# A Mamba, FFN, attention and MoE kernel: the first expert block's gate and up products beside the last chunk of the scan

## Chip, cores and metric

The kernel runs on one core of a Trainium2 chip. The metric is the device time of one execution in microseconds. Before the change: median 803.87 us of three runs (802.72 to 805.54). The engines are TensorE (PE in the profile), VectorE (DVE), ScalarE (ACT), GpSimd (POOL) and SyncE (SP, which here issues all DMAs).

## What is computed

Four layers, each as x = x + layernorm(layer(layernorm(x))), on x of 2 x 512 x 512 (b = batch). Only the first two are near the change:

```python
# layer 1: selective scan, 1024 channels of 16 states
state = state * exp(dt_t[..., None] * A) + (dt_t * u_t)[..., None] * B_t[:, None, :]
y = einsum('bdn,bn->bd', state, C_t)
out = ((y + x * D) * silu(gate)) @ W_out.T
# layer 2: FFN, 512 -> 1376 -> 512, 4 bit weights with scales s and zero points z (groups of 128)
w = q * s - (z + 1) * s          # for Wg, Wu and Wd
inter = silu(x2 @ Wg) * (x2 @ Wu)
out = (inter @ Wd).astype(float16)
```

Layer 3 is an attention over the 16 head dimensions of a token, layer 4 a MoE block whose experts are one shared weight, so that it comes down to products with folded weights.

## The kernel before

**The scan.** 1024 channels times two batches are 16 chunks of 128 channels (cc = 0 to 15, b = cc // 8). A chunk is 8 pairs (i = 0 to 127 in all, q = i % 8), and a pair is a 128 x 1024 tile of decays and states. Per pair ScalarE makes the decay by exp into PSUM (L1889), GpSimd the product dbu = rep_du * bc (L2397, up to three pairs ahead: it waits for the scan of pair i before the product of i + 3), VectorE the recurrence (`tensor_tensor_scan`, L1228), then VectorE (L1239) or, for two or three pairs of a chunk, GpSimd (L2406) the product with C, and TensorE sums two pairs at a time into the bank of y (L979). Once a chunk, one pair into the next chunk, VectorE multiplies y into the gate (`take_y`, L1255), for which TensorE then starts the next y with the product of u and D (L968).

**Other work in the scan** is put by hand. The table SIDE (L80) gives for chunk and pair of pairs what TensorE does ahead of its sums there; ScalarE and VectorE do their part of it a few pairs later (`pair_of(item) + n`). In chunks 13 and 14 stand the four transposes of the FFN's normalised input of batch 0 (`tr`, with `high_turned` on ScalarE and `low_turned` at L1318 on VectorE), in chunks 14 and 15 the partial output products of the scan layer (`part`, `take_partial`). In the last chunk `out_ahead` (L838) adds the second to last term of three output tiles, and `out_last` (L844) the last one behind the last `take_y`. All these products use a ring of three PSUM banks in the order of `pe_order` (L132).

**The FFN.** 1376 is padded to 11 blocks of 128 (IC). Weights are kept as two float16 halves, high and low, and a product is three matmuls (high x high, low x high, high x low, L721), 12 matmuls for a gate or up product of a block. Making a block's weights takes a chain: DMA of packed words, zero points and scales to one of four slots (`stage`, L627), `unpack` on VectorE (L1271), `whole` on ScalarE (cast to float16, L2163), then for blocks 0 and 1 `less_zero` (L1285) and products with scales split in two (`gate_up_halves`, `down_halves`, L1290 to L1296), and for the others `scaled` (L1278, L1280), `high_weights` on ScalarE (L2169) and `low_weights` on VectorE (L1300, L1305). In the pass of batch 0, TensorE does per block i gate and up, then the down product of block i - 1 (`down`, L992), which waits for `it_lo` (`ffn_low`, L1459). VectorE's order is written out: `unpack(0)`, `unpack(1)` and the last `take_y` close the scan (L1437), then L1560 to L1572, then the loop at L1573. `ffn_silu` (L2190), `ffn_times` (L1449) and `ffn_high` (L2197) stand between up product and `it_lo`. The next pass, of batch 1, uses the finished weights.

SyncE's queue has stage(0) in chunk 11, stage(1) behind the stores of wr, stage(2) behind the last `take_y`, stage(3) behind `out_last`, the others behind the low weights of the slot's user. Then come the loads for attention, bqraw among them (L674), and for the MoE block.

SBUF is laid out by hand in kilobytes (`at`, L209).

## Time and profile before

| | |
|---|---|
| median of three runs | 803.87 us |
| the profiled execution | 808.16 us, its span 806.3 us |
| mean granted TensorE clock | 0.907 of 2.4 GHz |
| busy: TensorE, VectorE, ScalarE, GpSimd | 689.0, 685.0, 469.9, 481.4 us |
| scan (VectorE's first to last) | 57.1 to 480.7 us |
| first gate product of the FFN | 489.7 us |
| last down product of its first pass | up to 579.1 us |

All times in the rows below are microseconds from the start of the span of this one execution, unless marked ns. A row of the timeline is: start, duration, engine, line of the kernel, operation, output and inputs by the program's names, shapes, count, and in brackets the idle time before it and what ended it. The granted clock is given as a share of 2.4 GHz; 0.50 is 1.2 GHz.

### The profile page before, as it was taken

The numbers are of one execution on the slowest core, as the hardware profiler recorded it, in microseconds if no ns is written. First come the engines' busy times: TensorE is split into PE (matmuls) and PEld (weight loads), VectorE is DVE, ScalarE is ACT, GpSimd is POOL, SyncE is SP. The second block draws the span as 40 slices with busy tenths as digits, with TensorE's granted clock in tenths as the row PEclk, the third lists the DMA queues.
The fourth block names the chain that finished last, engine by engine and source line by source line (L and its number), as shares of the span: only waits on it lengthen the run. The fifth ranks groups of instructions, "written<-read, shape, count | busy, mean of one in ns | idle before, by whom it ended". The sixth has DMA issues, their size and how long they took to land. (4 is left out here: it accounts for less than half of the span.)

```text
span 806.3 us, 8451 instructions
## 1 busy us (share of the span) xinstructions
PE 689.0 (85%) x2794; PEld 326.7 (41%) x2794; DVE 685.0 (85%) x697; ACT 469.9 (58%) x805; POOL 481.4 (60%) x252
## 2 busy tenths in 40 slices
PE   7979889987787799456646889999999999999995
PEld 7623333322122233111111224444444556887885
DVE  6879999999999989999999998999275575585778
ACT  5478768885656765867664546767235346323333
POOL 2429999999999999999999970220002014341130
PEclk9989979999788899856865988999999999999998
DMA  7533232335503705730334409973040030000011
GB/s 234 121 106 136 82 118 76 118 130 168 197 4 117 246 29 170 228 131 26 105 130 150 131 1 249 259 199 93 1 157 1 1 105 0 1 1 1 0 53 52
DMA packets 42358, 83.19 MB, mean 103 GB/s; under 512 B 6825, under 2 KB 10340, under 8 KB 42060
## 3 DMA queue, kind: packets, MB, share of 16 engines
q1 hardware_dynamic: 42316, 82.67, 32.4%
q8 instruction: 22, 0.36, 0.2%
q14 instruction: 20, 0.16, 0.1%
HBM read 71.44 MB, written 11.21 MB: 103 GB/s over the span
## 5 line engine op out<-in xcount | busy, mean ns | idle before, releaser
L2397 POOL TENSOR_TENSOR dbu<-rep_du,bc 128x1024 f32<-128x1024 f32 x127 | 296.5, 2361 | 2.5 <-DMA bc<-bc_scratch 1.2
L1889 ACT ACTIVATE psum<-rep_dt,aneg 128x512 f32<-128x512 f32 x256 | 166.3, 682 | 117.8 <-DVE hc L1239 96.3
L1228 DVE TENSOR_TENSOR_SCAN psum<-psum,dbu 128x1024 f32<-128x1024 f32 x89 | 203.3, 2285 | 3.0 <-ACT psum L1889 1.6
L979 PE MATMUL psum<-hc,stk 128*32 128x512 f32 x512 | 84.6, 743 | 54.5 <-POOL hc L2406 39.7
L1239 DVE TENSOR_TENSOR hc<-psum,bc 128x1024 f32<-128x1024 f32 x89 | 108.9, 1224 | 3.1
L2406 POOL TENSOR_TENSOR hc<-hc,bc 128x1024 f32<-128x1024 f32 x39 | 91.9, 2356 | 9.9 <-DVE hc L1228 9.9
L1228 DVE TENSOR_TENSOR_SCAN hc<-psum,dbu 128x1024 f32<-128x1024 f32 x39 | 88.9, 2280 | 5.5 <-PE psum L979 4.3
L718 PE MATMUL psum<-xf_hi,gu_hi 128*128 128x512 f16 x176 | 66.7, 379 | 0.1
L718 PE MATMUL psum<-xf_hi,gu_lo 128*128 128x512 f16 x176 | 66.7, 379 | 0.0
L718 PE MATMUL psum<-xf_lo,gu_hi 128*128 128x512 f16 x176 | 66.7, 379 | 0.0
L718 PE MATMUL psum<-xT,w_g 128*128 128x512 f32 x120 | 59.1, 641 | 2.6 <-ACT rep_du L2034 2.6
L2474 POOL TENSOR_TENSOR h<-h 128x512 f32<-128x512 f32 x16 | 19.4, 1213 | 68.0 <-ACT h L2305 68.0
L979 PEld LDWEIGHTS psum<-hc,stk 128*32 128x32 f32 x512 | 13.3, 120 | 109.8 <-issue 65.2
L968 PE MATMUL psum<-u,diag 128*32 128x512 f32 x128 | 23.5, 816 | 32.3 <-DVE u L1255 22.4
L2197 ACT CAST it_hi<-it 128x512 f16<-128x512 f32 x22 | 13.6, 618 | 48.1 <-DVE it L1449 48.0
L1449 DVE TENSOR_TENSOR it<-sg,psum 128x512 f32<-128x512 f32 x22 | 15.0, 684 | 29.2 <-PE psum L718 14.4
L718 PEld LDWEIGHTS psum<-xT,w_g 128*128 128x128 f32 x120 | 23.3, 204 | 40.0 <-issue 35.9
L2458 POOL TENSOR_TENSOR w_up_lo<-w_up,w_up_hi 128x1024 fp32r<-128x1024 f32 x4 | 9.4, 2388 | 46.2 <-ACT w_up_hi L2182 46.2
L718 PE MATMUL psum<-xT,w_x 128*128 128x512 f32 x64 | 32.6, 657 | 2.5 <-ACT xT L1773 2.0
L2445 POOL TENSOR_TENSOR x<-x,obuf 128x512 f32<-128x512 f32 x4 | 9.3, 2348 | 41.4 <-ACT obuf L1956 41.4
L1006 PE MATMUL psum<-d_hi,it_hi 128*128 128x512 f16 x88 | 33.3, 379 | 0.6 <-DVE it_lo L1459 0.6
L2452 POOL TENSOR_TENSOR w_gate_lo<-w_gate,w_gate_hi 128x32 fp32r<-128x32 f32 x1 | 0.7, 693 | 55.4 <-ACT w_gate_hi L2271 55.4
(301 smaller groups left out, 1455.2 us busy)
## 6 DMA issues: line engine op xcount, KB each, us to landing
rep_dt<-rep_scratch SPq DMA_DIRECT2D x60, 256.0 KB, 3.5
rep_du<-rep_scratch SPq DMA_DIRECT2D x60, 256.0 KB, 4.4
cw<-c_scratch SPq DMA_DIRECT2D x11, 768.0 KB, 8.1
qw<-qgu_in SPq DMA_DIRECT2D x11, 512.0 KB, 6.2
bc<-bc_scratch SPq DMA_DIRECT2D x16, 256.0 KB, 4.8
rep_scratch<-du_t SPq DMA_DIRECT2D x14, 256.0 KB, 2.0
rep_scratch<-dt_t SPq DMA_DIRECT2D x14, 256.0 KB, 2.3
qw<-qd_in SPq DMA_DIRECT2D x11, 256.0 KB, 7.1
```

Of the source, the lines that this page charges most:

```text
L718: last = pe.matmul(bank(item)[0:rows, cols], lhsT, rhs, start=(n == 0), stop=(n == len(parts) - 1))
L968: last = pe.matmul(y_rows(k), diag[:, k * P // KH:(k + 1) * P // KH], u[b][:, c, :], start=True, stop=False)
L979: last = pe.matmul(y_rows(k), stk[:], hc[:, (i + k // 2) % HCS, k % 2, :], start=False, stop=(s == GN - 1))
L1006: last = pe.matmul(psum[:, t, :], v, w, start=(i == 0 and n == 0), stop=(i == IC - 1 and n == 2))
L1228: dve.tensor_tensor_scan(h, a, dbu[:, i % DBS].rearrange("p e t -> p (e t)"), 0.0, ALU.mult, ALU.add)\
L1239: dve.tensor_tensor(hc[:, i % HCS], psum[:, two, :], bc[:, GN + n, :].unsqueeze(1).broadcast_to([P, 2, L]), ALU.mult)\
L1449: dve.tensor_tensor(it[:, k % 2, :], sg[:, k % 2, :], bank(("u", b, i)), ALU.mult)\
L1889: last = act.activation(psum[:, 2 * (i % 2) + e, :], rep_dt[:, cc % 2, k, :], ACT.Exp, scale=aneg[:, k, c, n:n + 1])
L2197: act.copy(it_hi[:, k % 2, :], it[:, k % 2, :]).then_inc(ithi_done, 1)
L2397: pool.tensor_tensor(dbu[:, i % DBS], rep_du[:, cc % 2, k:k + 2, :], bc[:, n, :].unsqueeze(1).broadcast_to([P, 2, L]), ALU.mult).then_inc( ...
L2406: pool.tensor_tensor(hc[:, i % HCS], hc[:, i % HCS], bc[:, GN + n, :].unsqueeze(1).broadcast_to([P, 2, L]), ALU.mult)\
L2474: pool.tensor_tensor(h2[:, k % 2, :], h1[:, k % 2, :], h1[:, k % 2, :], ALU.mult)\
```

## The change

The gate and up product of block 0, batch 0, move from the FFN's loop to chunk 15 of the scan. For that:

- VectorE does unpack(0) after pair 107 (13 * 8 + 3), less_zero(0) after 113, the two high halves of the gate and up weights after 115 and the low ones after 117. ScalarE casts the block's words after the decay of pair 110. The weights go to buffers of their own (hi_early, lo_early), since gu_hi and gu_lo of the block overlap buffers that the scan uses; so does the cast (q16_early).
- TensorE does the gate product ahead of the sums of pairs 120 and 121 and the up product ahead of those of 124 and 125. ScalarE copies the results to SBUF (sg_early, it_early) after pairs 124 and 127.
- After the scan: VectorE no longer unpacks block 0 there, and makes that block's down halves ahead of the last take_y. The order of the partial sums and weights of block 1 is another; the product of gate and up (times_early) comes between them. ScalarE's silu of block 0 runs from SBUF right after its table load.
- bqraw moves to another place in SBUF, and its load behind the wait for 10 releases of q16.

```diff
+UNPACK_AT = 13 * QP + 3
+WHOLE_AT = 13 * QP + 6
+HALVES_AT = 14 * QP + 1
@@ SIDE
-        (14, 1): [("part", 0)], (14, 2): [("part", 1)], (14, 3): [("part", 2)], (15, 1): [("part", 3)]}
+        (14, 1): [("part", 0)], (14, 2): [("part", 1)], (14, 3): [("part", 2)], (15, 0): [("g", 0, 0)],
+        (15, 1): [("part", 3)], (15, 2): [("u", 0, 0)]}
@@ buffers
+        q16_early = at("q16_early", 199, [SZ], F16)
+        hi_early = [at(f"hi_early{h}", k, [KH * P], F16) for h, k in enumerate([58, 170])]
+        lo_early = at("lo_early", 139, [2 * KH * P], F16)
+        sg_early = at("sg_early", 195, [L])
+        it_early = at("it_early", 197, [L])
-        bqraw = at("bqraw", 139, [DH, NH])
+        bqraw = at("bqraw", 203, [DH, NH])
@@ SyncE, behind the other loads for attention
+            sp_.wait_ge(q16_used, IC - 1)
+            load(bqraw[:].rearrange("p b c -> p (b c)"), bq_in.broadcast_to([P, DH * NH]), ld_att)
@@ TensorE, in the scan's loop
+                        if item[0] == "g":
+                            for t in range(NT):
+                                wait_taken(pe, ("tr", "ffn", 0, t))
+                            pe.wait_ge(whi_first, 1)
+                            pe.wait_ge(wlo_gu, 1)
+                        if item[0] in ("g", "u"):
+                            gate_or_up(*item)
@@ VectorE
+            def early_high():
+                for h in range(2):
+                    n = slice(h * KH * P, (h + 1) * KH * P)
+                    last = dve.tensor_tensor(hi_early[h][:], cw[0][:, 0, n], cw[0][:, 1, n], ALU.mult)
+                last.then_inc(whi_first, 1)
+
+            def early_low():
+                n = slice(0, 2 * KH * P)
+                dve.tensor_tensor(lo_early[:], cw[0][:, 0, n], cs[0][:, n], ALU.mult).then_inc(wlo_gu, 1)
+
+            def times_early():
+                dve.wait_ge(silu_early, 1)
+                wait_taken(dve, ("u", 0, 0))
+                dve.tensor_tensor(it_early[:], sg_early[:], it_early[:], ALU.mult).then_inc(it_done, 1)
...
+                if i == UNPACK_AT:
+                    unpack(0)
+                if i == HALVES_AT:
+                    less_zero(0)
+                if i == HALVES_AT + 2:
+                    early_high()
+                if i == HALVES_AT + 4:
+                    early_low()
...
-            unpack(0)
             unpack(1)
+            down_halves(0)
             take_y(NCH - 1)
...
-            less_zero(0)
-            gate_up_halves(0)
-            add_partial(0)
-            add_partial(1)
             less_zero(1)
             gate_up_halves(1)
+            add_partial(0)
+            times_early()
+            add_partial(1)
             add_partial(2)
+            down_halves(1)
             add_partial(3)
-            down_halves(0)
-            down_halves(1)
             unpack(2)
-            ffn_times(0, 0)
             scaled(2)
@@ ScalarE
+                if i == WHOLE_AT:
+                    whole(0)
+                if i == pair_of(("g", 0, 0)) + 4:
+                    take_early("g", sg_early)
+                if i == pair_of(("u", 0, 0)) + 3:
+                    take_early("u", it_early)
...
             act.wait_ge(exp_done, NPAIR)
             act.preload_act_table_set(SILU)
-            whole(0)
+            wait_taken(act, ("g", 0, 0))
+            act.activation(sg_early[:], sg_early[:], ACT.Silu).then_inc(silu_early, 1)
             whole(1)
```

## Rows read from the trace of the kernel before

**Rows 1.** Busy time by stretch: scan, closing matmuls, first FFN pass (columns as headed)
```profile
core 0: us, PE busy (x) PEld busy (x) DVE busy (x) ACT busy (x) POOL busy (x), PEclk, DMA share, GB/s
57.00:481.00 424.00, 326.65 (x1114) 105.88 (x1118) 412.43 (x252) 285.23 (x489) 409.39 (x200) 0.84 0.36 121
484.00:490.00 6.00, 6.00 (x10) 2.29 (x9) 4.96 (x9) 1.97 (x5) 0.00 (x0) 0.57 0.93 253
500.00:560.00 60.00, 58.96 (x275) 26.44 (x273) 56.51 (x65) 43.62 (x59) 9.32 (x4) 1.00 0.75 203
```

**Rows 2.** Timeline of TensorE and VectorE in the first FFN pass
```profile
500.07 0.38 PE L1006 MATMUL psum<-d_hi,it_hi 128*128 128x512 f16 x1
...
524.11 0.38 PE L1006 MATMUL psum<-d_hi,it_hi 128*128 128x512 f16 x1 [0.44 <-DVE it_lo L1459]
...
492.38 1.01 DVE L1271 TENSOR_SCALAR qw<-qw,shift 128x1536 int32<-128x1536 int32 x1
495.16 0.69 DVE L1449 TENSOR_TENSOR it<-sg,psum 128x512 f32<-128x512 f32 x1 [1.77 <-PE psum L718]
...
498.42 0.68 DVE L1459 TENSOR_TENSOR it_lo<-it,it_hi 128x512 f16<-128x512 f32 x1
```

**Rows 3.** The chain of waits, a gate and up product (start, us, what)
```profile
551.84 5.18 PE psum L718 x24
```

**Rows 4.** Costliest groups: GpSimd's product (busy us, mean ns, idle before)
```profile
L2397 POOL TENSOR_TENSOR dbu<-rep_du,bc 128x1024 f32<-128x1024 f32 x127 | 296.5, 2361 | 2.5 <-DMA bc<-bc_scratch 1.2
```

**Rows 5.** Timeline of VectorE behind the scan
```profile
480.64 1.94 DVE L1271 TENSOR_SCALAR qw<-qw,shift 128x1536 int32<-128x1536 int32 x2
...
483.19 0.96 DVE L1285 TENSOR_TENSOR cw<-q,cw 128x1536 f16<-128x1536 f16 x1
484.18 0.69 DVE L1290 TENSOR_TENSOR gu_hi<-cw 128x1024 f16<-128x1024 f16 x1
...
491.04 0.41 DVE L1295 TENSOR_TENSOR d_hi<-cw 128x512 f16<-128x512 f16 x1
```

**Rows 6.** Timeline of VectorE in chunks 13 to 15
```profile
414.05 1.22 DVE L1239 TENSOR_TENSOR hc<-psum,bc 128x1024 f32<-128x1024 f32 x1
...
435.22 0.66 DVE L1255 TENSOR_TENSOR u<-u,psum 128x512 f32<-128x512 f32 x1
...
474.99 2.29 DVE L1228 TENSOR_TENSOR_SCAN hc<-psum,dbu 128x1024 f32<-128x1024 f32 x1 [0.88 <-PE psum L979]
```

**Rows 7.** Timeline of GpSimd and VectorE, alone (429.81) and at the same time
```profile
429.81 1.27 POOL L2377 TENSOR_TENSOR du_t<-dt_t,u 128x512 f32<-128x512 f32 x1
...
518.83 4.58 POOL L2445 TENSOR_TENSOR x<-x,obuf 128x512 f32<-128x512 f32 x2 [39.14 <-ACT obuf L1956]
...
520.85 1.43 DVE L1271 TENSOR_SCALAR qw<-qw,shift 128x1536 int32<-128x1536 int32 x1
522.21 1.75 DVE L1459 TENSOR_TENSOR it_lo<-it,it_hi 128x512 f16<-128x512 f32 x1
```

**Rows 8.** Timeline of GpSimd in chunks 13 and 14
```profile
413.65 2.35 POOL L2406 TENSOR_TENSOR hc<-hc,bc 128x1024 f32<-128x1024 f32 x1
...
446.28 2.35 POOL L2406 TENSOR_TENSOR hc<-hc,bc 128x1024 f32<-128x1024 f32 x1 [1.18 <-DVE hc L1228]
```

**Rows 9.** Timeline of ScalarE: two casts behind the scan
```profile
481.68 2.85 ACT L2163 CAST q<-qw 128x1536 f16<-128x1536 int32 x2 [4.72 <-DVE qw L1271]
```

**Rows 10.** Timeline of TensorE in chunk 15 and behind it
```profile
462.87 1.93 PE L968 MATMUL psum<-u,diag 128*32 128x512 f32 x8 [3.01 <-DVE u L1255]
...
475.61 2.84 PE L838 MATMUL psum<-wout,u 128*128 128x512 f32 x6
480.77 1.07 PE L979 MATMUL psum<-hc,stk 128*32 128x512 f32 x8 [2.32 <-DVE hc L1239]
483.23 6.64 PE L844 MATMUL psum<-wout,u 128*128 128x512 f32 x8 [1.39 <-DVE u L1255]
```

**Rows 11.** Two stretches of 1 us, TensorE (busy us, granted clock, DMA share, GB/s)
```profile
462.00:463.00 1.00, 0.13 (x4) 0.50 0.00 0
468.00:469.00 1.00, 1.00 (x3) 0.65 0.00 0
```

More of the change, by code:

```diff
@@ L140, in pe_order @@
     for i in range(IC):
-        items += [("g", 0, i), ("u", 0, i)]
+        if i:
+            items += [("g", 0, i), ("u", 0, i)]
         if i >= TURN_FIRST:
@@ L303, in build, with high_of, low_of @@
         q16 = [at("q16_0", 149, [SZ], F16), at("q16_1", 203, [SZ], F16)]
+        q16_early = at("q16_early", 199, [SZ], F16)
[3 more added lines that the diff above has]
+        it_early = at("it_early", 197, [L])
+        def high_of(i, kk, j):
+            if i:
+                return gu_hi[:, i, (2 * kk + j) * P:(2 * kk + j + 1) * P]
+            return hi_early[kk // 2][:, (2 * (kk % 2) + j) * P:(2 * (kk % 2) + j + 1) * P]
+        def low_of(i, kk, j):
+            w = slice((2 * kk + j) * P, (2 * kk + j + 1) * P)
+            return gu_lo[:, i, w] if i else lo_early[:, w]
         xf_hi = [at(f"xf_hi{b}", k, [KH, L], F16) for b, k in enumerate([187, 195])]
@@ L673, in _ @@
             load(wqraw[:].rearrange("p a b c -> p (a b c)"), wq_in, ld_att)
-            load(bqraw[:].rearrange("p b c -> p (b c)"), bq_in.broadcast_to([P, DH * NH]), ld_att)
             load(wqkv[:, :, DH:QKV], wkv_in.rearrange("p (c k) -> p c k", c=KH), ld_att)
@@ L926, in y_rows, with gate_or_up @@
                 return psum[k * P // KH:(k + 1) * P // KH, Y_BANK, :]
+            def gate_or_up(name, b, i):
+                item = (name, b, i)
+                j = "gu".index(name)
+                start(item)
+                parts = []
+                for kk in range(KH):
+                    parts += halves(high_of(i, kk, j), low_of(i, kk, j), xf_hi[b][:, kk, :], xf_lo[b][:, kk, :])
+                product(item, parts).then_inc(work_ready, 1)
             for cc in range(NCH):
@@ L1011, in _ @@
                     k = b * IC + i
-                    if b == 0:
+                    if b == 0 and i:
                         if i < AHEAD:
-                            pe.wait_ge(whi_first, i + 1)
+                            pe.wait_ge(whi_first, i + 2)
                         pe.wait_ge(wlo_gu, i + 1)
                     for j, name in enumerate("gu"):
-                        item = (name, b, i)
-                        start(item)
-                        parts = []
-                        for kk in range(KH):
-                            w = slice((2 * kk + j) * P, (2 * kk + j + 1) * P)
-                            parts += halves(gu_hi[:, i, w], gu_lo[:, i, w], xf_hi[b][:, kk, :],
-                                            xf_lo[b][:, kk, :])
-                        product(item, parts).then_inc(work_ready, 1)
+                        if b or i:
+                            gate_or_up(name, b, i)
                         if b == 1 and j == 0 and i - 1 in TURN_BEHIND:
@@ L1284, in less_zero @@
                 dve.wait_ge(q16_done, i + 1)
-                dve.tensor_tensor(z, q16[i % 2][:], z, ALU.subtract).then_inc(q16_used, 1)
+                dve.tensor_tensor(z, q16[i % 2][:] if i else q16_early[:], z, ALU.subtract).then_inc(q16_used, 1)
                 dve.wait_ge(q16_used, i + 1)
+            def early_high():
[10 more added lines that the diff above has]
+                dve.tensor_tensor(it_early[:], sg_early[:], it_early[:], ALU.mult).then_inc(it_done, 1)
             def gate_up_halves(i):
@@ L1458, in ffn_low @@
                     dve.wait_ge(ffn_used, k - 1)
-                dve.tensor_tensor(it_lo[:, k % 2, :], it[:, k % 2, :], it_hi[:, k % 2, :],
+                dve.tensor_tensor(it_lo[:, k % 2, :], it[:, k % 2, :] if k else it_early[:], it_hi[:, k % 2, :],
                                   ALU.subtract).then_inc(itlo_done, 1)
@@ L2052, in take_wr, with whole, take_early @@
                 act.copy(wr_t[h][:], bank(item)).then_inc(taken_sem(item), 1)
+            def whole(i):
+                act.wait_ge(q_done, i + 1)
+                if i >= 2:
+                    act.wait_ge(q16_used, i - 1)
+                act.copy(q16[i % 2][:] if i else q16_early[:], qw[i % SLOTS][:]).then_inc(q16_done, 1)
+            def take_early(name, dst):
+                item = (name, 0, 0)
+                wait_work(act, item)
+                act.copy(dst[:], bank(item)).then_inc(taken_sem(item), 1)
             spread_dt_copy(0)
@@ L2156, in _ @@
                     own_root(("ffn", 0), fnmr, fnmr_ready)
-            def whole(i):
-                act.wait_ge(q_done, i + 1)
-                if i >= 2:
-                    act.wait_ge(q16_used, i - 1)
-                act.copy(q16[i % 2][:], qw[i % SLOTS][:]).then_inc(q16_done, 1)
             def high_weights(i):
@@ L2226, in _ @@
                 b, i = divmod(k, IC)
-                ffn_silu(k)
+                if k:
+                    ffn_silu(k)
                 if k == 0:
```

10 lines of the change are left out of this document (7 added, 3 removed).

## The prediction

> **What bounds the kernel now.** I read the busy time by stretches first [rows 1]. From 57 to 481 us (the scan) VectorE is busy 412 of 424 us and GpSimd 409, so both are full and VectorE, which must finish last, sets the end. From 500 to 560 us TensorE is busy 59 of 60 us, but VectorE 56.5 of 60. The second reading of that stretch matters more than the first: the first FFN pass is TensorE's only as long as VectorE, which makes the weights, keeps up, and one stall behind it_lo is there already [rows 2]. The chain of waits for the end of that pass has 24 matmuls of a gate and up product in 5.18 us [rows 3]; before them it steps back through VectorE and ScalarE. Next, the groups of instructions: GpSimd's 127 products of the scan take 2.36 us each, with both inputs in SBUF [rows 4], while every operation of VectorE in that stretch (L1228, L1239, L1247, L1255, L1318) takes one of its inputs from PSUM.
>
> **Part 1: VectorE's new work in the scan.** Four places get it: unpack(0) after pair 107, less_zero(0) after 113, early_high (two halves) after 115, early_low after 117. Alone [rows 5]: two unpacks take 1.94 us together, and consecutive instructions overlap by some 0.08, so one adds 0.93; less_zero 0.99 (483.19 to 484.18, with its wait on itself); each half of early_high 0.33 (d_hi has its shape, 0.41 less the overlap); early_low 0.61. Sum 3.19 us. Nothing hides it: VectorE is busy 97% of the scan [rows 1].
>
> The larger term is a wait. At 518.83 GpSimd starts two 128x512 sums that need 4.58 us, where such a product alone takes 1.27; in the same time VectorE's it_lo takes 1.75 us instead of 0.68 and the one before it, an unpack, 1.43 instead of 1.01 [rows 7, 2]. The numbers close if each stands still while the other runs: it_lo is issued at 522.21, GpSimd's second sum ends at 518.83 + 4.58 = 523.41, less some 0.1, and it_lo needs 0.68 from there and ends at 523.96. They take turns: the one that waited goes next. The Trainium skill ("SBUF — State Buffer", section "SBUF: two separate sides") has this as an exclusive lock on a port pair shared by VectorE (with two SBUF inputs, or in a two-port mode) and GpSimd. It speaks against this change, since all five new instructions are of that kind; by that rule as by the row the waits below are due, and without it the part would cost 3.18. The trace agrees (1.75 against 0.68).
>
> No VectorE instruction of the scan is of that kind today, and GpSimd is never idle long. So each new one waits for the rest of GpSimd's running product. From the rows [rows 6, 8], each shifted by what came before it:
> - unpack at 414.05 + 1.22 - 0.08 = 415.19: GpSimd's product runs from 413.65 to 416.0. Wait 0.77, total 1.7.
> - less_zero follows take_y (435.22, 0.66), 0.6 us behind the end of a scan that releases GpSimd's next product (2.35): wait 1.75 to 1.9, I take 1.85, total 2.84; sum 4.5.
> - early_high comes 1.2 us after the scan's end. GpSimd has caught up by then, because VectorE is 4.5 us late, and started on that end: wait 2.36 - 1.19 = 1.17. Its second half goes on at once, since GpSimd's next product needs a scan still to come, as at 446.28, where it waited 1.18 for one. Total 1.83; sum 6.4.
> - early_low: two GpSimd products back to back from the scan before; wait 1.3, total 1.9; sum 8.3.
>
> Bounds: 3.2 (no waits) to 5 x 2.36 + 3.2 = 15.0. I take 8.3, because the contended rows are of the very same instructions. ScalarE's cast at pair 110 (1.43 us: two take 2.85 [rows 9]) and its two copies in chunk 15 come right behind a decay, and the next decay waits for VectorE; ScalarE is busy 285 of 424 us [rows 1]: nothing, or under 1 us if a decay is late. SP loads nothing new in the scan; of its queue only the load of bqraw is moved, behind VectorE's tenth release of q16 (scaled(9), inside the first FFN pass); its reader comes in the second pass and behind it stand only the MoE loads: nothing.
>
> **Part 2: TensorE in chunk 15.** The gate product (12 matmuls, 2.59 us) goes into the idle time before take_y of chunk 14, which is 3.01 us now [rows 10] and some 6.5 with VectorE late, since the backlog that TensorE has there now is gone (an estimate: 3.0 and the 3.5 us between VectorE's product of pair 119 and its sums). It leaves 4 us idle, so the clock falls as before (0.50 at 462, back at 468.7, 5.8 us after TensorE resumed [rows 11]), and the 0.88 us wait of the scan of pair 126 stays [rows 6]. The up product follows the sums of pairs 122 and 123 at 474.7 (old times): 474.7 + 2.6 + 0.95 (sums of 124, 125) + 2.84 (out_ahead) = 481.1, so the last sums end at 482.2 instead of 481.84. Before take_y VectorE loses an unpack (0.93) and gains down_halves(0) (0.67). take_y starts at 482.25 instead of 482.50: 0.25 gained. A by-product: the idle 2.32 and 1.39 us on both sides of the last sums shrink to under 1, so the four closing matmuls run at 2.4 GHz, about 0.9 us each, and not 6.64 us together: they end at 486.5 instead of 489.7.
>
> **Part 3: the first FFN pass.** TensorE loses 24 matmuls, 5.18 us [rows 3], and 3.2 us of the slow clock: 8.4 us if it set the pace. It doesn't. It must next have it_lo of block 0, then the low weights of block 2. VectorE's list up to unpack(2): take_y ends at 482.9; ScalarE's cast makes less_zero(1) start at 483.1; then 0.99 + 1.2 (halves of 1) + 4 x 0.6 (partials) + 0.6 (times_early) + 0.7 (down_halves(1)) = 489.0. The transfer of block 2 (1.5 MB at some 253 GB/s, started with take_y [rows 1]) ends near 489.9. So unpack(2) is at 489.9 instead of 492.38, the cast follows, and scaled(2) starts at 492.4 instead of 495.8, since it no longer stands behind the product of 495.16, which waited 1.77 us for TensorE [rows 2]. it_lo(0) ends 495.7. The shift of the weight chain stays between 2.9 (transfers: 6.2 us per block) and 3.4: I take 3.2.
>
> TensorE is done with block 1 at 492.4, idles 3.3 us, and by the 3.01 us case its clock falls for 5.8 us, which costs 2.9. down(0) stood at 500.07; it starts at 495.7 and is worth 4.4 - 2.9 = 1.5 us. Then TensorE regains the 1.05 us of stalls between 500 and 560 [rows 1], not VectorE's limit of 3.2: 2.5 us gained (ends: 0, and 8.4).
>
> **Sum**: +8.3 - 0.25 - 2.5 = +5.5 us. The profiled execution took 808.16 (span 806.3 and 1.9 around it), 4.3 above the median of 803.87; added to the median: 809.4 us. A measurement of this kernel tells 0.3% (2.4 us) from no change.
>
> **Rivals.**
> A. The port costs nothing in the scan: GpSimd's 1024-element products may let VectorE in. For: no row shows these two together in the scan. Against: rows 7. Then 3.2 - 0.25 - 2.5 = +0.5: 804.4. Chance 0.15.
> B. Faster: TensorE, and not the weight chain, sets the pace of the first FFN pass. For: it is busy 59 of 60 us. Against: the stall behind it_lo and VectorE's 56.5. Worth 8.4 instead of 2.5; it wins by the measurable 2.4 us once the scan part is below 6.2, and at 3.2 it gives 3.2 - 0.25 - 8.4 = -5.5: 798.4. With the waits of the scan paid in full it ends at -0.4, no change. Chance of the faster end 0.09.
> C. Worse: GpSimd lags instead of having caught up, so that each of the five instructions meets a fresh product, early_high's second half too. +15.0 - 0.25 - 2.5 = +12.2: 816.1. Against: products released by the scan's end. Chance 0.10.
> D. The products are early but the pass doesn't start earlier (gain 0, scan 8.3): +8.1, 812. Inside the upper part of my range.
>
> **How the numbers follow.** Forecast with D 0.66; A 0.15; B 0.09; C 0.10. The forecast's own range is 807 to 812.5 (waits of 4 to 7 us, gain of 0 to 3.2). With most of A it is 803.2 to 812.5. Slower by over 0.3%: 0.66 + 0.10 less a tail = 0.74; same: A and that tail, 0.17; faster 0.09.
>
> **What would show it.** Right: in chunks 13 and 14 the new VectorE rows are longer than alone (less_zero near 2.8 instead of 0.96) and the last scan starts 8 us later; L844's matmuls take under 4 us; TensorE idles 3 us before down(0), whose it_lo ends it; unpack(2) near 490 in old times. Wrong: the new rows have 0.9, 0.95, 0.4, 0.7 us (then A), or TensorE has no idle time between block 1 and down(0) and the pass ends over 6 us nearer to take_y (then B).

## The result, and the profile after

The changed kernel takes 812.88 us (median of 4 runs, 809.58 to 815.19). The kernel before, in the same comparison, takes 804.52 (4 runs, 802.72 to 805.54). The ratio is 1.0102, with a 95% interval of 1.0073 to 1.0131: slower by 8.2 us, between 5.9 and 10.5. The forecast of 809.4 had the right sign and was too low; the time lies 0.4 us above the range. The four runs of the changed kernel stand in two pairs (809.58 and 810.84, 814.91 and 815.19), and the median lies in the gap between them, so these 0.4 us alone say little; which step failed is read from the profiles.

The two profiled executions are only 2.7 us apart (810.84 against 808.16). The profiled execution of before contains a stall of TensorE in chunk 8, long before the change, that the one of after does not. In the timeline of TensorE of the kernel after, the sums of one pair and the 16 output products behind them:

```profile
277.22 1.07 PE L1018 MATMUL psum<-hc,stk 128*32 128x512 f32 x8 [2.83 <-POOL hc L2475]
278.22 7.13 PE L741 MATMUL psum<-wout,g 128*128 128x512 f32 x16
```

The same two in the profile of before:

```profile
278.48 1.94 PE L979 MATMUL psum<-hc,stk 128*32 128x512 f32 x8 [3.09 <-POOL hc L2406]
280.34 9.13 PE L718 MATMUL psum<-wout,g 128*128 128x512 f32 x16
```

And the scan of VectorE that waits behind those products, before (ahead of it 3.38 us idle):

```profile
290.63 2.29 DVE L1228 TENSOR_TENSOR_SCAN hc<-psum,dbu 128x1024 f32<-128x1024 f32 x1 [3.38 <-PE psum L979]
```

and after (0.27 us idle):

```profile
286.51 2.29 DVE L1261 TENSOR_TENSOR_SCAN hc<-psum,dbu 128x1024 f32<-128x1024 f32 x1 [0.27 <-PE psum L1018]
```

So the spans cannot be set against each other as they are. I cut both executions at instructions that they share, and read the start of each from VectorE's timeline (us):

| stretch | before | after | difference |
|---|---|---|---|
| first scan | 57.10 | 56.82 | -0.28 |
| first scan to scan of pair 104 | 344.90 | 341.10 | -3.80, of which 3.1 is the stall above |
| scan of pair 104 to the last scan | 75.19 | 82.84 | **+7.65** |
| last scan to block 0's product `it` of the second token block | 107.13 | 106.17 | **-0.96** |
| that product to the end of the span | 221.98 | 221.97 | -0.01 |

The part that the change can reach is +7.65 - 0.96 = +6.7 us. The last scan starts at 480.76 and the second `it` at 586.93, against 477.19 and 584.32.

**Chunks 13 to 15.** VectorE's timeline of the kernel after, the new instructions with the one that follows each (columns: start us, us, engine, line, operation, out<-in, forms, count, idle before and its releaser):

```profile
411.14 1.63 DVE L1304 TENSOR_SCALAR qw<-qw,shift 128x1536 int32<-128x1536 int32 x1
412.69 0.68 DVE L1366 TENSOR_TENSOR xf_lo<-psum,xf_hi 128x512 f16<-128x512 f32 x1
...
433.29 2.75 DVE L1318 TENSOR_TENSOR cw<-q_early,cw 128x1536 f16<-128x1536 f16 x1
436.08 0.69 DVE L1366 TENSOR_TENSOR xf_lo<-psum,xf_hi 128x512 f16<-128x512 f32 x1
...
443.61 1.88 DVE L1324 TENSOR_TENSOR hi_early<-cw 128x512 f16<-128x512 f16 x2
445.41 0.68 DVE L1366 TENSOR_TENSOR xf_lo<-psum,xf_hi 128x512 f16<-128x512 f32 x1
...
451.65 1.94 DVE L1329 TENSOR_TENSOR lo_early<-cw,cs 128x1024 f16<-128x1024 f16 x1
453.51 2.28 DVE L1261 TENSOR_TENSOR_SCAN hc<-psum,dbu 128x1024 f32<-128x1024 f32 x1
...
480.76 2.30 DVE L1261 TENSOR_TENSOR_SCAN psum<-psum,dbu 128x1024 f32<-128x1024 f32 x1 [0.51 <-POOL dbu L2466]
```

From start to start the four take 1.55, 2.79, 1.80 and 1.86 us, where the same work alone takes 0.93, 0.99, 0.66 and 0.61 [rows 5]. The 2.79 can be followed to the tenth in GpSimd's timeline of the same kernel:

```profile
432.87 2.36 POOL L2475 TENSOR_TENSOR hc<-hc,bc 128x1024 f32<-128x1024 f32 x1 [0.34 <-DVE hc L1261]
435.19 3.07 POOL L2466 TENSOR_TENSOR dbu<-rep_du,bc 128x1024 f32<-128x1024 f32 x1
```

less_zero is issued at 433.29. GpSimd's product ends at 432.87 + 2.36 = 435.23. less_zero ends at 433.29 + 2.75 = 436.04, some 0.8 behind it, which leaves room for its own 0.96 less the overlap; and GpSimd's next product, issued at 435.19, takes 3.07 instead of 2.36, since now it is the one that stands. None of these waits is printed in brackets: the profile counts the time as busy. It shows only as a duration that is too long.

**Behind the scan.** Two windows that answer to [rows 1] (PE, PEld, DVE, ACT, POOL busy, granted clock, DMA share, GB/s):

```profile
484.00:492.00 8.00, 6.07 (x22) 2.02 (x22) 7.69 (x14) 3.21 (x6) 0.00 (x0) 1.00 0.47 119
500.00:560.00 60.00, 57.46 (x259) 25.37 (x260) 56.53 (x65) 44.10 (x61) 9.34 (x4) 0.97 0.74 212
```

VectorE's timeline of the kernel after, from take_y of the last chunk (485.83; 482.50 before) to block 0's it_lo [rows 2, 5]:

```profile
485.83 0.68 DVE L1288 TENSOR_TENSOR u<-u,psum 128x512 f32<-128x512 f32 x1
486.78 0.96 DVE L1318 TENSOR_TENSOR cw<-q,cw 128x1536 f16<-128x1536 f16 x1 [0.27 <-ACT q L2112]
...
492.05 0.68 DVE L1613 TENSOR_TENSOR obuf<-psum,obuf 128x512 f32<-128x512 f32 x1
495.76 1.02 DVE L1304 TENSOR_SCALAR qw<-qw,shift 128x1536 int32<-128x1536 int32 x1 [3.03 <-DMA cw<-c_scratch]
498.36 0.96 DVE L1311 TENSOR_TENSOR cw<-q,cw 128x1536 f16<-128x1536 f16 x1 [1.58 <-ACT q L2112]
...
501.03 0.68 DVE L1515 TENSOR_TENSOR it_lo<-it_early,it_hi 128x512 f16<-128x512 f32 x1
```

and TensorE's from chunk 15 on [rows 10, 2]:

```profile
466.81 1.78 PE L1007 MATMUL psum<-u,diag 128*32 128x512 f32 x8 [3.76 <-DVE u L1288]
...
484.37 1.06 PE L1018 MATMUL psum<-hc,stk 128*32 128x512 f32 x8 [0.32 <-DVE hc L1272]
486.56 2.84 PE L867 MATMUL psum<-wout,u 128*128 128x512 f32 x6 [1.13 <-DVE u L1288]
489.72 1.12 PE L867 MATMUL psum<-wout,u 128*128 128x512 f32 x2 [0.32 <-DVE obuf L1613]
...
501.86 0.58 PE L1045 MATMUL psum<-d_hi,it_hi 128*128 128x512 f16 x1 [5.51 <-DVE it_lo L1515]
```

Two things are to be seen. TensorE now has 5.51 us of idle time ahead of down(0), where it had none. And VectorE, which should have gone on to unpack(2), waits 3.03 us for the transfer of block 2: unpack(2) starts 9.93 us behind take_y, in the kernel before 9.88 (492.38 - 482.50). The work taken out of this stretch left a hole: measured from the start of the last scan, unpack(2) comes 0.19 us sooner and block 0's it_lo 0.96 us sooner (20.27 against 21.23), which is the whole gain of the pass.

It is the whole gain because nothing behind that point changed. From block 2's it_lo to the end of the "pass" in the table takes 69.40 to 69.48 us in the profiles of all fourteen kernels, whatever TensorE's clock and idle time were before. The pass is decided in the first 34 to 39 us behind the start of the last scan.

### The profile page after: what moved, and what is told of

It is laid out like the page before. It is cut to its first block and busy times, and to the rows that moved or that the text cites. A ratio compares the mean times of both kernels' runs of the same rounds, so it can differ in the third digit from the quotient of the medians.

```text
span 808.9 us, 8456 instructions
## 1 busy us (share of the span) xinstructions
PE 681.1 (84%) x2794; PEld 323.9 (40%) x2794; DVE 689.9 (85%) x698; ACT 471.0 (58%) x807; POOL 483.7 (60%) x252
## 5 line engine op out<-in xcount | busy, mean ns | idle before, releaser
L1018 PE MATMUL psum<-hc,stk 128*32 128x512 f32 x512 | 81.9, 717 | 58.7 <-POOL hc L2475 39.7
L741 PE MATMUL psum<-xf_hi,gu_hi 128*128 128x512 f16 x160 | 60.7, 379 | 0.2 <-DVE obuf L1613 0.2
L741 PE MATMUL psum<-xf_lo,gu_hi 128*128 128x512 f16 x160 | 60.6, 379 | 0.0
L741 PE MATMUL psum<-xf_hi,gu_lo 128*128 128x512 f16 x160 | 60.6, 379 | 0.0
L1045 PE MATMUL psum<-d_hi,it_lo 128*128 128x512 f16 x88 | 33.9, 385 | 0.0
L1045 PE MATMUL psum<-d_lo,it_hi 128*128 128x512 f16 x88 | 33.9, 385 | 0.0
```

The lines of the kernel that those rows point to most:

```text
L741: last = pe.matmul(bank(item)[0:rows, cols], lhsT, rhs, start=(n == 0), stop=(n == len(parts) - 1))
L1018: last = pe.matmul(y_rows(k), stk[:], hc[:, (i + k // 2) % HCS, k % 2, :], start=False, stop=(s == GN - 1))
L1045: last = pe.matmul(psum[:, t, :], v, w, start=(i == 0 and n == 0), stop=(i == IC - 1 and n == 2))
```

## The experiments

The theory on record had two terms: VectorE waits for the port behind GpSimd's products in the scan (rival A says it does not), and the weight chain limits the first FFN pass (rival B says TensorE does). After the result the open question was why the pass gives so little; the new theory was the transfer of block 2, which starts only with take_y. "Scan" and "pass" below are two stretches of the table above, from the scan of pair 104 to the last scan and from there to the second token block's first product. Each ratio is to runs of the kernel before in the same comparison; their median was 803.85 to 805.61 us.

| run | scan | pass | median | ratio to before (95%) |
|---|---|---|---|---|
| before | 75.19 | 107.13 | | |
| after | 82.84 | 106.17 | 812.88 | 1.0102 (1.0073 to 1.0131) |
| e1 weights only | 83.05 | 106.95 | 812.79 | 1.0106 (1.0067 to 1.0144) |
| e2 grouped | 79.86 | 105.07 | 807.78 | 1.0049 (1.0024 to 1.0075) |
| e3 transfer early | 82.81 | 103.70 | 810.01 | 1.0085 (1.0055 to 1.0115) |
| e4 e2 and e3 | 79.85 | 104.86 | 807.74 | 1.0050 (1.0027 to 1.0073) |
| e5 before, transfer early | 74.83 | 105.27 | 804.02 | 0.9991 (0.9962 to 1.0020) |
| e6 before, 8 sums, one input PSUM | 79.99 | 108.08 | 810.41 | 1.0076 (1.0044 to 1.0107) |
| e7 before, 8 sums, both SBUF | 84.67 | 106.50 | 815.46 | 1.0130 (1.0097 to 1.0163) |
| e8 group behind the scan | 80.68 | 105.20 | 810.09 | 1.0072 (1.0044 to 1.0101) |
| e9 e8, e3, split loads | 80.71 | 104.60 | 807.51 | 1.0032 (1.0012 to 1.0051) |
| e10 before, clock kept | 75.25 | 105.88 | 805.74 | 1.0011 (0.9991 to 1.0031) |
| e11 e10, e3, split loads | 75.24 | 105.60 | 803.87 | 0.9990 (0.9968 to 1.0011) |
| e12 e2, e3, split, clock kept | 79.86 | 103.40 | 805.55 | 1.0017 (1.0001 to 1.0032) |

### e6 and e7: what the port costs in the scan

Both are the kernel before with the same sum placed eight times between a scan and its product with C. Only its first input differs. The sums are added work, and nothing uses what they give.

```diff
+DUMMY_AT = (107, 108, 110, 111, 112, 115, 117, 119)
...
                 scan(i)
+                if i in DUMMY_AT:
+                    dve.wait_ge(scan_done, i + 1)
...
+                    dve.tensor_tensor(dummy[:], psum[:, 2 * (i % 2), :], x[:, 1, :], ALU.add)   # e6
+                    dve.tensor_tensor(dummy[:], x[:, 0, :], x[:, 1, :], ALU.add)                # e7
                 if not on_pool(i):
                     times_c(i)
```

> The kernel before with eight more VectorE additions of 128x512 float32 between a scan and its product with C, in chunks 13 and 14, one input in PSUM and one in SBUF; their results are not used. Theory (they don't meet GpSimd) and rival alike: 8 x 0.6 to 0.7 = 5 us slower, every one of them 0.68 us long.

> The same eight additions with both inputs in SBUF. Theory (such an instruction and GpSimd's product run one after the other): most of them wait for the rest of a product of 2.36 us, 1 to 2.3 us each, so that the eight cost 12 to 22 us and not 5, and GpSimd's idle time grows. Rival (port or not, the cost is VectorE's own time): as with one input in PSUM, 5 us, each 0.68 us long.

The view of one tile (durations in ns: shortest, median, longest), first of e6:

```profile
L1433 DVE TENSOR_TENSOR dummy<-psum,x x8: 690/691/691, 413.6 to 457.8; 128x512 f32<-128x512 f32 x8
```

then of e7:

```profile
L1433 DVE TENSOR_TENSOR dummy<-x x8: 693/933/2495, 412.8 to 460.5; 128x512 f32<-128x512 f32 x8
```

With one input in PSUM every sum takes 0.69 us, whatever GpSimd does at the time; the stretch is 4.80 us longer, 0.60 for each. With both in SBUF it is 9.48 us longer, 1.19 for each. Where the first input lies is the only difference, and it costs 4.7 us for eight. The whole runs point the same way: +0.76% against +1.30%, with intervals that touch near 1.01. That decides against rival A. The Trainium skill ("SBUF — State Buffer", section "SBUF: two separate sides") says that a VectorE operation with two SBUF inputs takes the shared port pair for itself against a GpSimd operation that reads SBUF, and whichever starts first blocks the other; the eight rows of either kernel agree.

The size was a miss: e7's text expected 12 to 22 us and waits of 1 to 2.3 us for most sums. Only three of the eight waited that long (2.50, 1.87 and 1.85 us long); one took 1.11 and four 0.69 to 0.76, because both engines were ready at nearly the same time, at the end of a scan, and VectorE went first. VectorE's timeline of e7 shows both sides:

```profile
412.75 2.50 DVE L1433 TENSOR_TENSOR dummy<-x 128x512 f32<-128x512 f32 x1
...
436.38 0.69 DVE L1433 TENSOR_TENSOR dummy<-x 128x512 f32<-128x512 f32 x1
```

and GpSimd's, for the second of them:

```profile
436.43 2.85 POOL L2406 TENSOR_TENSOR dbu<-rep_du,bc 128x1024 f32<-128x1024 f32 x1 [1.21 <-DVE psum L1232]
```

At 436.4 it is GpSimd that pays, 2.85 instead of 2.36; GpSimd had been idle for 1.21, so that costs the scan little.

### e1: the products alone

The kernel after, but block 0's gate and up products are back in the FFN, and take_early, times_early and the early silu are taken out again. The weights are still made in the scan. The diff shows the main lines.

```diff
-        (14, 1): [("part", 0)], (14, 2): [("part", 1)], (14, 3): [("part", 2)], (15, 0): [("g", 0, 0)],
-        (15, 1): [("part", 3)], (15, 2): [("u", 0, 0)]}
+        (14, 1): [("part", 0)], (14, 2): [("part", 1)], (14, 3): [("part", 2)], (15, 1): [("part", 3)]}
...
-        if i:
-            items += [("g", 0, i), ("u", 0, i)]
+        items += [("g", 0, i), ("u", 0, i)]
```

> The changed kernel with the gate and up products of block 0 back in the FFN; VectorE's and ScalarE's weight work stays in chunks 13 and 14. Theory (the scan pays about 8.0 us for VectorE's five instructions, and the early products themselves are worth under 1.5 us, because the first FFN pass starts with the transfer of block 2 and then runs at VectorE's pace): within 1.5 us of the changed kernel, 7 to 9.5 us above the kernel before. Rival (TensorE sets the pace of the pass, the products are worth 5 us or more): 5 to 8 us above the changed kernel.

The median is that of the kernel after within 0.1 us, the pass 106.95 against 106.17: as the theory said. But the 0.8 us is not the price of the 24 matmuls (5.18 us of TensorE's work [rows 3]), for two other things differ in this profile. Block 2 lands 1.5 us sooner behind its release than in the kernel after, so unpack(2) waits only 0.25 us. And now it is TensorE that holds the chain. VectorE's timeline of e1, block 0's product of gate and up:

```profile
499.18 0.69 DVE L1495 TENSOR_TENSOR it<-sg,psum 128x512 f32<-128x512 f32 x1 [3.25 <-PE psum L739]
```

and TensorE's, the closing matmuls ahead of the gate and up products:

```profile
487.18 6.71 PE L865 MATMUL psum<-wout,u 128*128 128x512 f32 x8 [1.12 <-DVE u L1278]
```

So the gain and the wait change places: in e1 TensorE holds block 0, in the kernel after the transfer does. The clean price of the early products needs both kernels without either, and e11 and e12 give it below: 2.2 us, not the 8.4 of rival B.

The closing matmuls took 4.0 us in the kernel after (2.84 + 1.12) and take 6.7 here, but the early products do not decide that. Where TensorE idled 0.3 to 0.4 us ahead of the last sums (after, e2, e3, and e5, which has the list of the kernel before), they took 4.0 us; where it idled 2.0 to 2.4 us (before, e1, e6, e7, and e4, e8, e9, which have the early products), 5.1 to 6.7. Both orders of work stand on both sides. What differs is when out_ahead was done: 3.2 to 3.3 us behind the start of the last scan in the first group, 1.2 to 1.6 in the second. The by-product that the forecast named came about in this execution; it does not belong to the change.

### e3: the transfer of block 2 as soon as the last scan is done

```diff
-            sp_.wait_ge(y_taken, NCH)
+            sp_.wait_ge(scan_done, NPAIR)
             stage(2)
```

> The changed kernel with the transfer of block 2 started when the last scan is done and not when the last take_y is. Theory (the first FFN pass waits for this transfer): the transfer starts 3 us sooner, unpack(2) starts at the end of VectorE's list, its idle 3.0 us is gone, and the pass ends 2.5 to 3 us sooner: 2.5 to 3 below the changed kernel. Rival (the pass is held by TensorE or by ScalarE's casts and norms): under 1 us.

VectorE's timeline of e3:

```profile
492.59 1.01 DVE L1304 TENSOR_SCALAR qw<-qw,shift 128x1536 int32<-128x1536 int32 x1
495.18 0.96 DVE L1311 TENSOR_TENSOR cw<-q,cw 128x1536 f16<-128x1536 f16 x1 [1.58 <-ACT q L2112]
...
499.76 1.02 DVE L1304 TENSOR_SCALAR qw<-qw,shift 128x1536 int32<-128x1536 int32 x1 [1.23 <-DMA cw<-c_scratch]
```

and TensorE's:

```profile
498.68 0.38 PE L1045 MATMUL psum<-d_hi,it_hi 128*128 128x512 f16 x1 [2.39 <-DVE it_lo L1515]
```

The wait of 3.03 us ahead of unpack(2) is gone, down(0) has 2.39 us idle time ahead of it instead of 5.51, and the pass is 2.5 us shorter than in the kernel after (103.70 against 106.17). So the transfer held it. Block 2 landed 4.9 us sooner behind the last scan. Of these 3.4 are the edit, more than the wait of 3.03, and 1.5 are that it landed 7.7 us behind its release in this profile and not 9.2. One line further the next wait shows: unpack(3) waits 1.23 us for block 3. In the runs e3 is at 1.0085, and its interval holds the 1.0102 of the kernel after, so the 2.5 us stand on the profile.

The same edit alone, in the kernel before, is e5:

> The kernel before with the transfer of block 2 started when the last scan is done. Theory: there VectorE's list reaches unpack(2) when the transfer has landed, so that it costs nothing: within 0.7 us of the kernel before. Rival (the transfer holds that kernel's pass too): 2 us or more faster.

The ratio is 0.9991 (0.9962 to 1.0020): too little to tell from no change, as the theory said. The pass is 1.86 us shorter in the profile, but it was not the transfer that held the profile of before. In the kernel before block 2 had landed 1.45 us before VectorE came to unpack(2), as the view of DMA issues shows below, so that starting it earlier had nothing to give. What differs is TensorE's clock. TensorE's timeline of e5, where the kernel before took 6.64 us [rows 10]:

```profile
478.70 4.03 PE L844 MATMUL psum<-wout,u 128*128 128x512 f32 x8 [1.39 <-DVE u L1255]
```

and VectorE's wait for TensorE ahead of block 0's product, 1.77 us before [rows 2]:

```profile
488.02 0.69 DVE L1449 TENSOR_TENSOR it<-sg,psum 128x512 f32<-128x512 f32 x1 [0.21 <-PE psum L718]
```

The granted clock over these matmuls is 1.00 in e5 and 0.50 before. So the one profile of before shows its pass with the slow closing matmuls, and another execution with the same list on TensorE and VectorE is 1.9 us shorter there. With the fast closing matmuls VectorE comes to unpack(2) sooner, and only then the transfer begins to matter: e10, which has them without the early transfer, waits 0.54 us for it.

### e2, e8: where in the scan the weights are made

e2 is the kernel after with the three steps together after pair 115, behind its product with C.

```diff
-                if i == HALVES_AT:
-                    less_zero(0)
                 if i == HALVES_AT + 2:
+                    less_zero(0)
                     early_high()
-                if i == HALVES_AT + 4:
                     early_low()
```

> The changed kernel with less_zero, early_high and early_low together after pair 115. Theory (each of them waits for GpSimd's running product, and GpSimd has nothing to run until the next scan ends): one wait of some 1.2 us instead of 1.8 + 1.2 + 1.2; the four instructions take 0.99 + 0.66 + 0.61 + 1.2 = 3.5 us instead of 6.5, the scan ends 3 us sooner, 2.5 to 3.2 us below the changed kernel. Rival (VectorE's instructions are slow in the scan for another reason, their number and size decide): as the changed kernel, within 0.8 us.

VectorE's timeline of e2:

```profile
441.62 2.17 DVE L1318 TENSOR_TENSOR cw<-q_early,cw 128x1536 f16<-128x1536 f16 x1
443.83 0.76 DVE L1324 TENSOR_TENSOR hi_early<-cw 128x512 f16<-128x512 f16 x2
444.51 0.68 DVE L1329 TENSOR_TENSOR lo_early<-cw,cs 128x1024 f16<-128x1024 f16 x1
```

and GpSimd's next product of states:

```profile
448.07 2.35 POOL L2473 TENSOR_TENSOR hc<-hc,bc 128x1024 f32<-128x1024 f32 x1 [5.09 <-DVE hc L1261]
```

One wait (2.17 instead of 0.96) is paid for four instructions. The others run alone, because GpSimd has used up what the scans had released and waits for a new scan, 5.09 us in all. The scan is 2.98 us shorter, and the runs follow: 1.0049 against 1.0102. That is the part of the loss that the placement alone made. Its pass is 1.1 us shorter too, but that is not the grouping: block 2 landed 1.1 us sooner behind the last scan in this execution (unpack(2) at 13.89 us instead of 15.00). The medians differ by 5.1 us, more than the 2.5 to 3.2 expected and more than the 4.1 of the two stretches.

e8 puts the same group right behind scan 115, ahead of its product with C.

```diff
                 scan(i)
+                if i == HALVES_AT + 2:
+                    less_zero(0)
+                    early_high()
+                    early_low()
                 if not on_pool(i):
                     times_c(i)
... (their three old places further down are emptied)
```

> The changed kernel with less_zero, early_high and early_low together right behind the scan of pair 115 and ahead of its product with C, where GpSimd waits for that scan too. Theory (whoever has the port first keeps it for one instruction, and GpSimd has caught up by then): the wait of 1.2 us of the grouped version shrinks to under 0.3, GpSimd's next product is the late one, the scan's last 24 pairs take 78.6 to 79.2 us instead of 79.9 (grouped) and 82.8 (changed), 807 us in all. Rival (the place doesn't matter once they are grouped): 79.9.

VectorE's timeline of e8:

```profile
439.60 1.12 DVE L1318 TENSOR_TENSOR cw<-q_early,cw 128x1536 f16<-128x1536 f16 x1
440.76 2.78 DVE L1324 TENSOR_TENSOR hi_early<-cw 128x512 f16<-128x512 f16 x2
```

and GpSimd's:

```profile
435.24 7.69 POOL L2464 TENSOR_TENSOR dbu<-rep_du,bc 128x1024 f32<-128x1024 f32 x3
```

A miss. less_zero now gets in with 1.12, as hoped, but the two halves take 2.78, 2.0 more than in e2: GpSimd had one more product ready, took its turn between VectorE's instructions (three products in 7.69 us instead of 7.08), and VectorE stood behind it. The stretch is 0.8 us longer than e2's. A wait for the port is not avoided by getting in first; it is avoided when GpSimd has no work at hand, as in e2.

### e4, e9, e12: what is left when the repairs are put together

e4 is e2 and e3. e9 is e8 and e3, and unpack waits for the quantised weights alone, while less_zero and scaled wait for the constants (main line of the edit; the constants get a semaphore of their own):

```diff
-                dve.wait_ge(ld_stage[s], 48 * (i // SLOTS + 1) + (16 if s < AHEAD else 0))
+                dve.wait_ge(ld_stage[s], 32 * (i // SLOTS + 1))
```

e12 is e2, e3 and this split, with keep_clock(4) behind out_ahead and again ahead of the closing matmuls. keep_clock issues short products with the identity whose results are not used. In e9 and e11 the split and the early transfer come together; no run has the split alone.

> Both edits on the changed kernel. Theory: they add up, 5 to 6 us below the changed kernel, and so 0.5 to 2.5 us above the kernel before, a difference that is hard to tell from none. Rival (either lever is not real): 3 us or less below the changed kernel.

> The version before it, with the transfer of block 2 started when the last scan is done, and with unpack waiting for the packed words alone (zero points and scales have a semaphore of their own, for which less_zero and scaled wait). Theory (the first FFN pass of the changed kernel is held by the transfers of blocks 2 and 3, cw last): no idle time of VectorE for a transfer before unpack(2) and unpack(3); from the last scan to the first product of the next pass 103 us or less (before 107.1, changed 106.2, early transfer 103.7). With 79 for the last 24 pairs that is about the kernel before: 803 to 806 us. Rival (the earlier transfers don't add up, VectorE's and ScalarE's chain holds the pass at 104 to 105): 806 to 808.

> The changed kernel with everything that helped: less_zero, early_high and early_low together behind pair 115, the early transfer of block 2, unpack waiting for the packed words alone, and eight small dummy products in TensorE's idle stretches around the last sums, so that the closing matmuls run at 2.4 GHz. Theory: the last 24 pairs take 79.9 us (one wait for the port) and the way from the last scan to the first product of the next pass 103 to 103.7 us, together 183 to 183.6 where the kernel before has 182.3: 0.5 to 1.5 us above it, within what can be told from no change. So even then the early products don't pay for VectorE's work in the scan. Rival (the pass gains the full 8.4 us of TensorE's saved time once transfers and clock are out of the way): the way takes 99 us, 3 us below the kernel before.

TensorE's timeline of e12, ahead of down(0):

```profile
500.69 0.38 PE L1049 MATMUL psum<-d_hi,it_hi 128*128 128x512 f16 x1 [2.46 <-DVE it_lo L1519]
```

and VectorE's, on the way to it:

```profile
494.53 1.01 DVE L1308 TENSOR_SCALAR qw<-qw,shift 128x1536 int32<-128x1536 int32 x1
497.19 0.96 DVE L1316 TENSOR_TENSOR cw<-q,cw 128x1536 f16<-128x1536 f16 x1 [1.65 <-ACT q L2116]
```

No transfer is waited for any more, TensorE's clock is up, and TensorE idles 2.46 us behind the chain unpack, cast, scaled, it_lo. The pass is 103.40, as the theory said, and not 99, as the rival did. Like is to be set against like here: e11 is the kernel before with the same three repairs, and its pass is 105.60. So the early products and the work they take off VectorE's list are worth 2.2 us of the pass, once transfers and clock are out of the way. The scan costs 79.86 - 75.24 = 4.6, which leaves +2.4 in the profiles, and the runs agree (1.0017 against 0.9990, some 2.2 us). Against the kernel before as it was, the best version with early products is at +0.9 in the profile and 1.0017 (1.0001 to 1.0032) in the runs.

e4 shows that gains of the parts do not simply add: with its transfer early, unpack(3) waited 2.30 us for block 3, its pass (104.86) is only 0.2 us below e2's, and its median is e2's. It was expected 5 to 6 us below the changed kernel and is 5.1 below, but e2 alone gives as much. e9 is a miss: neither unpack waits for a transfer, as expected, but the pass is 104.60 and not 103, and the median 807.51 and not 803 to 806. That is where its rival put it. Among what differs from e12's profile: the closing matmuls took 6.31 us there, and VectorE waits 0.98 us for one of them.

### e10, e11: the clock alone, in the kernel before

```diff
                         for t in range(NT - 1):
                             out_ahead(t)
+                        pe.wait_ge(scan_done, NPAIR - 1)
+                        keep_clock(6)
...
+            keep_clock(4)
             pe.wait_ge(y_taken, NCH)
```

e11 has in addition the edit of e3 and the split waits of e9.

> The kernel before with ten small dummy products on TensorE in the two idle stretches around the last sums. Theory (the closing four matmuls run at 1.2 GHz because of these stretches, and VectorE's product of block 0 waits 1.77 us for TensorE behind them): they take 4.0 us instead of 6.6, the pass ends 1.5 us sooner, 1 to 2 us below the kernel before. Rival (the pass is VectorE's or the transfers' anyway): within 0.5 us.

> The same dummy products, the early transfer of block 2 and unpack waiting for the packed words alone, all on the kernel before. Theory: 1.5 to 3 us below the kernel before, the fastest of all, since nothing is added to the scan. Rival: as the dummy products alone.

TensorE's timeline of e10:

```profile
478.14 1.50 PE L862 MATMUL psum<-ident 128*128 128x128 f32 x12
...
483.08 4.03 PE L844 MATMUL psum<-wout,u 128*128 128x512 f32 x8 [0.30 <-DVE u L1258]
```

The closing matmuls take 4.03 us instead of 6.64 [rows 10]. The pass is 1.25 us shorter in e10's profile and 1.5 in e11's, near the 1.5 expected; the runs cannot tell either from no change, so the 1 to 2 us and 1.5 to 3 us expected of the whole times are not confirmed. None of the twelve kernels is faster than the kernel before by a measurable amount.

## Why the prediction was right in part, and where it failed

**Part 1, the scan: right, to the instruction.** Forecast 1.7, 2.84, 1.83 and 1.9 us, 8.3 in all; measured 1.55, 2.79, 1.80 and 1.86, 8.0 in all. Against the 8.0 stands a stall of 0.88 us ahead of the scan of pair 126 that the forecast kept and that is gone, and one of 0.51 us ahead of the last scan, behind GpSimd, that is new; the stretch is 7.65 us longer. The five instructions are 3.2 of it. Rivals A (0.5 in all) and C (each wait a whole product) are out, by these rows and by e6 against e7. The places fit too: ahead of each new instruction GpSimd's product runs as the forecast had it, and early_high's second half goes on at once, with GpSimd idle for 3.49 us behind. Nothing else was late: ScalarE's cast and copies added no wait, as forecast.

**Part 2, TensorE in chunk 15: right in its times, partly by luck.** take_y starts 0.24 us closer to the last scan (forecast 0.25). TensorE idles 3.76 us between the gate product and take_y of chunk 14 (forecast 4). The closing matmuls take 4.0 us instead of 6.64, but e4, e8 and e9, with the same list on TensorE, took 5.1 to 6.3: that they ran at 2.4 GHz in the profiled execution was luck. Of the idle times around the last sums, both forecast to be under 1 us, one is (0.32) and one is not (1.13). The forecast that the stall of 0.88 stays was wrong.

**Part 3, the first FFN pass: the step that failed.** "The transfer of block 2 (1.5 MB at some 253 GB/s, started with take_y [rows 1]) ends near 489.9." It had 7.0 us from the end of take_y. Measured, it is 9.2: take_y ends at 486.5, and unpack(2), which waits for it, starts at 495.76, 15.0 us behind the start of the last scan, where the forecast had 12.7. SyncE's timeline of the kernel after shows that it is not the start that is late:

```profile
486.53 0.54 SPq L528 DMA_DIRECT2D qw<-qgu_in  x1
...
487.76 0.59 SPq L528 DMA_DIRECT2D cw<-c_scratch  x1
```

The view of DMA issues, in a window that holds only the three loads of block 2, has the time from issue to landing as its last column. The last load of the three, before (window 483.1 to 485; issued at 484.43) and after (486.4 to 488; issued at 487.76):

```profile
cw<-c_scratch SPq DMA_DIRECT2D x1, 768.0 KB, 6.5
cw<-c_scratch SPq DMA_DIRECT2D x1, 768.0 KB, 8.0
```

So block 2 landed 7.7 us behind its release before (at 490.9) and 9.2 us after. Of the 2.2 us that the forecast missed, 0.7 is the way it was worked out: bytes by the rate of a stretch, where what counts is the wait in the queue (the last load is issued 1.2 us behind the first) and then its own time. This part could be read from the trace of before, where no wait shows it, since VectorE came to unpack(2) only at 492.38. The other 1.5 us is a transfer that took longer in the kernel after. It goes together with the next transfer. Block 3's is released at the end of the closing matmuls, 6.7 us behind block 2's before and 4.3 us after, when those matmuls were fast. In the five profiles where block 3 followed within 6 us (after, e2, e7, e8, e10), block 2 took 8.1 to 9.2 us; in the nine where it followed later, 7.7 to 8.1. No run changed the release of block 3 alone, so that the one slows the other is argued and not shown.

That unpack(2) starts 9.9 us behind take_y in both kernels is a coincidence: VectorE's list set it before, the landing after. With it the shift of the weight chain is not "between 2.9 and 3.4" but 0.96: 0.19 at unpack(2), and the rest because scaled(2) no longer stands behind the product of 495.16. The forecast then went on with TensorE's account (down(0) 4.4 sooner, less 2.9 for the clock, plus 1.05 of stalls). That account had no place: TensorE's clock did fall (0.50 from 501.8 to 504.4, behind an idle time of 5.51 us instead of 3.3), and the pass still shows the shift of it_lo(0), 0.96, unchanged to its end.

In the terms of the sum: 0.25 and 2.5 were forecast for what follows the last scan, 2.75 together, and 0.96 came, 1.8 too little; the scan came 0.65 lower than forecast. The step that failed is thus the transfer's time and what was hung on it, and it accounts for 1.8 us. The sum of the profiles, +6.7, would have stayed inside the range, and +1.1 us of the 3.5 between 809.4 and 812.88 is what the two stretches missed together. Another 0.65 is that the kernel before has a median of 804.52 in this comparison and not 803.87; the rest is open, below. The forecast had the case of no gain as rival D, 812, without a chance of its own; D's place was right.

**What stays open.** The sum of the two terms is +6.7 us, and the runs say +8.2 (5.9 to 10.5). The missing 1.5 lies within the interval. In 12 of the 13 kernels, though, the difference of the medians is above the sum of the two stretches, by 1 us in the middle (e6 alone is below, by 0.9). One and the same profile of before stands in all of those sums, and e5 shows what may be behind it: with fast closing matmuls the pass of that order of work is 105.27 and not 107.13. Set against e5's two stretches the kernel after is at +8.9, so that +6.7 and +8.9 enclose what the runs say, and the gain of the pass, 0.96 against the one profile, may be none against the other. How often the kernel before runs either way is not known, as it was profiled once.

## What to carry to other kernels

Before work is moved from a stretch into a full engine's time, find out what else holds that stretch, transfers first: work that hides a landing shows no wait, so read each later load's landing from the view of DMA issues, in a window that holds it alone, and ask how much earlier its reader would come. Ask also which transfer a faster stretch releases sooner. Where two engines share a port, price an instruction by the partner's running instruction, not by its own duration; move it to a place where the partner has nothing ready, and put such instructions together. Where one execution's time depends on chance stalls elsewhere, set profiles side by side in stretches between shared instructions, never span against span, and set a version with repairs against the kernel before with the same repairs.

## What the runs showed that was not expected

- A transfer of block 2 (three loads, 1.5 MB) needed 7.7 to 9.2 us from the release to the landing in the fourteen profiles, where bytes by the rate of [rows 1] give 6.2.
- The same kernel's order of work gives TensorE different clocks in different executions at the same place. In chunk 8, behind idle times of 3.09 and 2.83 us, eight sums took 1.94 us (before, granted clock 0.50 there, 1.2 GHz) or 1.07 (after, 1.00, 2.4 GHz), the products behind them 9.13 or 7.13, and a scan was late by 3.4 us or 0.3. In the profiles the stretch up to pair 104 comes out near 341 us (after, e1 to e5, e8 and e9) or near 344.5 (before, e6, e7, e10), with e11 and e12 in between. The runs of some kernels stand in two groups as well (those of the kernel after as said above, e3's at 808.35 to 810.01 and 813.97 to 814.58), and the profiled executions with the short stretch were mostly among the faster half of their kernel's runs (after, e2, e3, e5, e8, e9); that these are the same thing is not shown.
- When VectorE and GpSimd are both ready at the end of a scan, either may go first: the shortest of e7's sums took 0.69 us and the longest 2.50.
- In none of these profiles is a wait for the port printed as idle time with a releaser. A duration that is too long, in either engine's rows, is all that shows it.
